# Sorted expert layers: the slot's token is found by one-hot products and its row gathered, where the token's row was scattered to its slot

## Chip, cores and metric

One core of one Trainium2 chip runs the whole program. The metric is the device time of one execution in microseconds (us); for the kernel before, the median of three runs.

## The reference, cut to what matters

`x` has 8 x 256 tokens of 128 numbers. Four times a cross attention and then a feed-forward layer are added to it, each with a gate. The change touches the feed-forward layers 1 and 2, which have eight experts with 512 hidden units:

```python
# layer 1: one expert per token, weighted by its probability
route = softmax(xn @ router_w + router_b); best = argmax(route)
a, g = split(xn @ w1[best], 2);  y = silu(a) * g @ w2[best]
x = x + tanh(g_ffn[1]) * y * max(route)
# layer 2: two experts per token, weighted by the softmax of the two logits
vals, idx = top_k(xn @ gate_w + gate_b, 2); share = softmax(vals)
y_k = gelu(xn @ w1[idx_k] + b1[idx_k]) @ w2[idx_k] + b2[idx_k]
x = x + tanh(g_ffn[2]) * sum_k share_k * y_k
```

`xn` is the layer norm of `x`.

## The kernel before

The five engines have programs of their own and meet at semaphores. The function `sparse_ffn` is called for layer 1 (`gated`, K = 1) and layer 2 (K = 2); below they are stage 1 and stage 2. `x` lies in SBUF as 16 tiles of 128 tokens.

**Sorting.** VectorE and GpSimd make the layer norm (lines 2522 to 2537, 2291), TensorE transposes it and makes the router's logits (2311, 2319). VectorE finds the expert of each token, TensorE counts the tokens of each expert and ranks them (2326 to 2331), and VectorE turns that into a slot number for each token (2593 to 2607). Each expert owns whole tiles of 128 slots; there are NS = 24 tiles in stage 1 and 40 in stage 2, which suffices for every outcome. Their owners are computed in 2608 to 2611 and loaded into TensorE's registers (2356).

**Rows to slots.** A DRAM scratch per layer holds rows of 130 numbers: the normalised token, its number, its share. It is filled with empty rows (number 1.0e6) at the start of the first attention, by 16 transfers of 260 KB on SP's queue (536). After `rows_done`, GpSimd scatters 128 rows at a time with indirect DMAs (2297): 16 in stage 1, 32 in stage 2, where ScalarE first copies the rows (2450) since the second choice has other numbers in its last columns. When all have landed, SP fetches groups of four tiles in slot order (2269), up to three ahead; group `g` goes into buffer `g % 3`.

**Weights.** SP loads the experts one by one into a ring of 2 (stage 1) or 3 (stage 2) raw buffers (2257 to 2263); ScalarE rounds them to f16 (`high`, 2435) and VectorE writes what is left (`low`, 2542, 2544). The first RING experts come before the routing on VectorE, the others after it (2619). In stage 2, VectorE's matrix of shares (2618), its transposition (2337), ScalarE's copy (2452), the product with the second bias (2347) and the addition to `x` (2627) stand there too, and TensorE goes on only when that is added.

**Loop.** NG = 6 or 10 groups of 4 tiles, 4 chunks of 128 hidden units each. TensorE transposes a fetched group (`turn`, 2368), multiplies with the owner's weights (`chunk`, 2376 to 2378) and multiplies back (`result`, 2407 to 2411). ScalarE and VectorE split the transposed rows and the hidden values into two f16 parts each. `turn(g + 2)` comes in the middle of group `g`; every product is three matmuls. In stage 2 a chunk passes VectorE (bias, 2653), ScalarE (gelu 2478, high part 2485) and VectorE (low part, 2661). VectorE copies token numbers and shares out of each fetched group (2636, 2637), ScalarE scales the result by the share (2493, four instructions), and GpSimd scatters it by token number into `results` (2303), four indirect DMAs per group; empty slots are left out by the bound check. Once all have landed, SP brings the results back in four quarters (2275) and VectorE adds them to `x` (2689, 2691).

```python
for g in range(NG):
    pool.wait_ge(token_done, 2 * (g + 1))
    pool.wait_ge(y_done, g + 1)
    for i in range(GT):
        nc.gpsimd.indirect_dma_start(results, ...token_at...)
```

## Time and profile before

| | us |
|---|---|
| three runs | 2479.51, 2480.14, 2485.76 |
| median | 2480.14 |
| profiled execution | 2482.54 |
| its span | 2480.80 |
| PE, DVE, ACT, POOL busy | 2031.9, 1742.9, 1339.0, 531.4 |
| mean granted TensorE clock | 0.893 |

PE is TensorE, PEld its weight loads, DVE VectorE, ACT ScalarE, POOL GpSimd, SP the engine that only issues DMAs; a q behind a name (SPq, PEldq) is that engine's sequencer. Times in rows are us from the span's start unless ns is said. A timeline row has start, duration, engine, line, operation, output<-input, and in brackets how long the engine sat idle before it and what ended that. "xN" is a number of instructions.

### The profile page before, as it was taken

How to read it: one execution, taken by the hardware profiler on the slowest of the kernel's cores; microseconds unless marked ns; L12 is line 12 of the kernel's file. 1: busy time of each engine (PE TensorE's matmuls, PEld its weight loads, DVE VectorE, ACT ScalarE, POOL GpSimd, SP SyncE). 2: the span in 40 equal slices, each digit the busy share in tenths (PEclk: the TensorE clock that was granted, in tenths of full speed). 3: DMA queues.
4: the chain of work that ended last, by engine and by line, in shares of the span. 5: the costliest groups of instructions: out<-in, count | busy, mean ns of one | idle time of the engine just before them, and what ended most of it. 6: DMA issues, size and time to landing. Idle time of an engine off the chain costs nothing. (4 is left out here: it accounts for less than half of the span.)

```text
span 2480.8 us, 47937 instructions
## 1 busy us (share of the span) xinstructions
PE 2031.9 (82%) x17000; PEld 1395.1 (56%) x17001; DVE 1742.9 (70%) x3576; ACT 1339.0 (54%) x1775; POOL 531.4 (21%) x510
## 2 busy tenths in 40 slices
PE   3699636999984949999999999999547389999677
PEld 3434324888864715555555555556436268888544
DVE  2567365888875457788787877876535468888688
ACT  1247314777753416666666666667335257777321
POOL 2100001000002323434443344435433300000010
PEclk9679766999996959999999999999668689999789
DMA  5311100000004010000000000000211100000000
GB/s 143 57 24 11 23 0 1 0 0 0 0 27 120 19 49 9 9 12 9 12 9 11 11 9 12 9 11 4 84 54 40 40 1 0 0 0 0 1 22 24
DMA packets 94870, 53.74 MB, mean 22 GB/s; under 512 B 43517, under 2 KB 88808, under 8 KB 94358
## 3 DMA queue, kind: packets, MB, share of 16 engines
q1 hardware_dynamic: 86516, 42.51, 7.3%
q0 software_dynamic: 3584, 6.36, 0.8%
q10 hardware_dynamic: 4610, 2.71, 0.5%
q8 instruction: 104, 1.70, 0.3%
q14 instruction: 56, 0.46, 0.1%
HBM read 30.16 MB, written 13.75 MB: 18 GB/s over the span
## 5 line engine op out<-in xcount | busy, mean ns | idle before, releaser
L1446 POOL TENSOR_TENSOR aw_p_lo<-aw_p,aw_p_hi 128x512 f16<-128x512 f32 x256 | 303.1, 1184 | 499.6 <-ACT aw_p_hi L1400 499.5
L1482 DVE TENSOR_REDUCE aw_max_part<-ps 128x1 f32<-128x512 f32 x512 | 349.8, 686 | 77.2 <-PE ps L1275 74.4
L1398 ACT ACTIVATE aw_p<-ps 128x1024 f32<-128x1024 f32 x256 | 262.3, 1024 | 260.2 <-PE ps L1307 260.1
L1324 PE MATMUL ps<-ctx_hi_lo,aw_p_hi 128*128 128x194 f16 x2048 | 290.8, 247 | 1.2 <-DVE aw_p_lo L1494 0.7
L1494 DVE TENSOR_TENSOR aw_p_lo<-aw_p,aw_p_hi 128x512 f16<-128x512 f32 x256 | 267.5, 1045 | 22.0 <-ACT aw_p_hi L1400 22.0
L1327 PE MATMUL ps<-ctx_hi_lo,aw_p_lo 128*128 128x97 f16 x2048 | 279.4, 207 | 0.0
L1400 ACT ACTIVATE aw_p_hi<-ps 128x1024 f16<-128x1024 f32 x256 | 260.5, 1018 | 0.0
L1275 PE MATMUL ps<-ctxT_hi,aw_queries 96*128 96x512 f16 x512 | 204.1, 400 | 36.0 <-DVE aw_max_part L1482 35.4
L1327 PEld LDWEIGHTS ps<-ctx_hi_lo,aw_p_lo 128*128 128x128 f16 x2048 | 200.4, 98 | 26.1
L1324 PEld LDWEIGHTS ps<-ctx_hi_lo,aw_p_hi 128*128 128x128 f16 x2048 | 199.7, 98 | 5.0 <-issue 4.0
L1302 PE MATMUL ps<-aw_queries,aw_keys 128*128 128x512 f16 x512 | 194.5, 380 | 0.3 <-ACT aw_p_hi L1400 0.3
L1303 PE MATMUL ps<-aw_queries,aw_keys 128*128 128x512 f16 x512 | 193.9, 379 | 0.0
L1040 ACT ACTIVATE at_p<-ps 128x1024 f32<-128x1024 f32 x128 | 131.1, 1024 | 102.9 <-PE ps L946 102.9
L1098 DVE TENSOR_REDUCE at_neg_max<-ps 128x2 f16<-128x512 f32 x256 | 174.3, 681 | 6.0 <-PE ps L925 5.6
L1122 DVE SCALAR_TENSOR_TENSOR x_res<-ps,at_rden,x_res 128x128 f32<-128x128 f32 x520 | 158.6, 347 | 9.2
L447 POOL TENSOR_TENSOR ln_rstd<-ln_var_eps,neg_half 128x16 f32<-128x16 f32 x6 | 17.6, 2932 | 687.3 <-DVE ln_var_eps L433 653.2
L969 PE MATMUL ps<-C,u_out 97*128 (+1 forms) x1040 | 160.2, 276 | 5.1 <-DVE x_res L1122 5.1
L1128 DVE TENSOR_TENSOR at_p_lo<-at_p,at_p_hi 128x1024 f16<-128x1024 f32 x128 | 155.6, 1216 | 7.9 <-ACT at_p_hi L1042 7.7
L969 PEld LDWEIGHTS ps<-C,u_out 97*128 97x128 f32 x1040 | 136.2, 191 | 11.6 <-DVE x_res L1122 8.3
L956 PE MATMUL ps<-at_p_hi,ctx_hi_lo 128*128 128x256 f16 x512 | 140.9, 275 | 1.1 <-DVE at_p_lo L1128 1.1
L944 PE MATMUL ps<-at_q_hi,ctxT_hi 97*128 97x256 f16 x512 | 141.6, 277 | 0.0
L945 PE MATMUL ps<-at_q_hi,ctxT_lo 96*128 96x256 f16 x512 | 141.5, 276 | 0.0
(377 smaller groups left out, 4687.3 us busy)
## 6 DMA issues: line engine op xcount, KB each, us to landing
sf_weights_raw<-in_L_w SPq DMA_DIRECT2D x24, 256.0 KB, 4.1
slot_scratch<-at_empty_rows SPq DMA_DIRECT2D x16, 260.0 KB, 8.1
sf_fetched<-slot_scratch SPq DMA_DIRECT2D x16, 260.0 KB, 3.0
sf_weights_raw<-in_L_w SPq DMA_DIRECT2D x8, 512.0 KB, 3.8
x_norm<-result_scratch SPq DMA_DIRECT2D x8, 256.0 KB, 4.2
aw_queries<-aw_queries SPq DMA_DIRECT2D x32, 64.0 KB, 1.9
aw_queries<-aw_q_lo SPq DMA_DIRECT2D x32, 64.0 KB, 2.0
raw<-in_L_q SPq DMA_DIRECT2D x3, 512.0 KB, 10.4
```

The lines of the kernel that those rows point to most:

```text
L969: ins = nc.tensor.matmul(ps[:, BANKS[b], t * (CW + 1):(t + 1) * (CW + 1)], M.U[:, upar, (2 * half + t) * P:(2 * half + t + 1) * P], C[:, s ...
L1098: nc.vector.tensor_reduce(nmax[:, par, 2 * k:2 * k + 2], ps[:, BANKS[b], :].rearrange("p (t k) -> p t k", t=2), AX.X, ALU.max, negate=True ...
L1275: nc.tensor.matmul(ps[:, bank, :], S1[0:DC, b % 4, t * P:(t + 1) * P], M.ct_hi[0:DC, kb * QB:(kb + 1) * QB], start=True, stop=True).then_i ...
L1302: nc.tensor.matmul(o, K1[:, ks], S1[:, c, :], start=True, stop=False)
L1303: nc.tensor.matmul(o, K2[:, ks], S2[:, c, :], start=False, stop=False)
L1324: nc.tensor.matmul(ps[:, bank, at:at + 2 * VW - 2], p_hi[:, n % 3, cols], M.cv[:, kt, 0:2 * VW - 2], start=kt == 0 and t % 2 == 0, stop=False,
L1327: ins = nc.tensor.matmul(ps[:, bank, at:at + DA], p_lo[:, n % 3, cols], M.cv[:, kt, 0:DA], start=False, stop=kt == NT - 1, skip_group_chec ...
L1398: nc.scalar.activation(p[:, n % 2, :].rearrange("p (b q) -> p b q", b=2), s, ACT.Exp, scale=1.0 / QS).then_inc(p_done, 1)
L1400: nc.scalar.activation(p_hi[:, n % 3, :].rearrange("p (b q) -> p b q", b=2), s, ACT.Exp, scale=1.0 / QS).then_inc(hi_done, 1)
L1446: nc.gpsimd.tensor_tensor(p_lo[:, n % 3, QB:], p[:, n % 2, QB:], p_hi[:, n % 3, QB:], ALU.subtract).then_inc(lo_b, 1)
L1482: nc.vector.tensor_reduce(mpart[:, b % 2, k:k + 1], ps[:, bank, :], AX.X, ALU.max).then_inc(m_done, 1)
L1494: nc.vector.tensor_tensor(p_lo[:, n % 3, 0:QB], p[:, n % 2, 0:QB], p_hi[:, n % 3, 0:QB], ALU.subtract).then_inc(lo_a, 1)
```

## The change

The rows stay in token order: SP stores the normalised rows to a DRAM scratch `rows`, ahead of the load of expert RING. VectorE cuts each slot number into a tile (`>> 7`) and a place in the tile (`& 127`), and makes two f16 one-hot sets: `in_part` (place) and `in_tile` (tile, times token number + 1). TensorE multiplies them, so that `found` holds token + 1 for each slot, or 0. VectorE makes two address lists: `token_at` (0 for empty slots) and `home_at` (beyond the bound for empty slots, + 2048 for second choices). GpSimd gathers the rows of group `g` by `token_at`, three groups before the loop and group `g + 3` ahead of the scatter of result `g`. The shares are no longer carried with the rows: ScalarE copies the result in one instruction, and VectorE multiplies by the share when it adds. The empty rows, their transfers and ScalarE's copy of the rows go, as do the token and share copies in the loop. Rows have 128 numbers in place of 130, and `combT` shares `M.xt`'s memory. The declarations of semaphores and the slices `0:D` that became `:` are left out here:

```diff
@@ -36,7 +36,7 @@
...
-XW = D + 2
+XW = D
@@ -113,9 +113,8 @@
...
-    M.count = sb("count", [P, 1, 64], F32)
-    M.slots = {n: nc.dram_tensor(f"slot_scratch{n}", [k * P, XW], F32, kind="Internal").ap()
-               for n, k in ((1, 24), (2, 40))}
+    M.count = sb("count", [P, 1, P], F32)
+    M.rows = nc.dram_tensor("row_scratch", [NTOK, D], F32, kind="Internal").ap()
@@ -268,7 +267,7 @@
...
-    link(nc.gpsimd.iota(M.count[:], [[1, 64]], base=0, channel_multiplier=0,
+    link(nc.gpsimd.iota(M.count[:], [[1, P]], base=0, channel_multiplier=0,
@@ -498,8 +497,6 @@
...
-        empty = sb("empty_rows", [P, TQ, XW], F32)
@@ -524,17 +521,9 @@
...
-    nc.gpsimd.memset(empty[:], 0.0).then_inc(empty_zeroed, 1)
-    pool.wait_ge(empty_zeroed, 1)
-    nc.gpsimd.memset(empty[:, :, D:D + 1], 1.0e6).then_inc(empty_done, 1)
...
-    sp.wait_ge(empty_done, 1)
-    for n, k in ((1, 24), (2, 40)):
-        for i in range(k // TQ):
-            sp.dma_start(M.slots[n][i * QB:(i + 1) * QB, :].rearrange("(t p) f -> p t f", p=P), empty[:]
-                         ).then_inc(cleared, 16)
@@ -544,7 +533,6 @@
...
-    sp.wait_ge(cleared, 64 // TQ * 16)
@@ -2177,7 +2165,7 @@
...
-    ps, slots, results = M.ps, M.slots[layer], M.results
+    ps, rows, results = M.ps, M.rows, M.results
@@ -2209,10 +2197,15 @@
...
-        slot_at = sb("slot_at", [P, K, NT], mybir.dt.uint32)
-        fetch = sb("fetched", [P, 3, GT, XW])
-        token_at = sb("token_at", [P, 4, GT], mybir.dt.uint32)
-        share_at = sb("share_at", [P, 4, GT])
+        slot_int, part_int = (sb(n, [P, K, NT], mybir.dt.int32) for n in ("slot_int", "part_int"))
+        slot_part, slot_tile = (sb(n, [P, K * NT]) for n in ("slot_part", "slot_tile"))
+        in_part = sb("in_part", [P, K * NT, P], F16)
+        in_tile = sb("in_tile", [P, K * NT, NS], F16)
+        token1 = sb("token1", [P, NT], F16)
+        found = sb("found", [P, K, NS])
+        token, home, none = (sb(n, [P, NS]) for n in ("token", "home", "none"))
+        token_at, home_at = (sb(n, [P, NS], mybir.dt.uint32) for n in ("token_at", "home_at"))
+        fetch = sb("fetched", [P, 3, GT, D])
@@ -2223,27 +2216,28 @@
...
-            combT = sb("combT", [E, NTOK])
+            combT = M.xt[0:E, :]
...
-        rows = [M.xn, M.xt_rows]
@@ -2256,23 +2250,22 @@
...
+        if e == RING:
+            for q in range(NQ):
+                sp.wait_ge(normed, (q + 1) * TQ)
+                sp.dma_start(rows[q * QB:(q + 1) * QB, :].rearrange("(t p) f -> p t f", p=P),
+                             M.xn[:, q * TQ:(q + 1) * TQ, :]).then_inc(rows_stored, 16)
...
-    sp.wait_ge(scattered, K * NT * 16)
-    for g in range(NG):
-        if g >= 3:
-            sp.wait_ge(s_turned, g - 2)
-            sp.wait_ge(token_done, 2 * (g - 2))
-        sp.dma_start(fetch[:, g % 3], slots[g * QB:(g + 1) * QB, :].rearrange("(t p) f -> p t f", p=P)
-                     ).then_inc(fetched[g % 3], 16)
+    sp.wait_ge(rows_stored, 4 * 16)
...
-            sp.dma_start(sum_of[k][:, q * TQ:(q + 1) * TQ, 0:D],
+            sp.dma_start(sum_of[k][:, q * TQ:(q + 1) * TQ, :],
@@ -2282,25 +2275,35 @@
...
-    nc.gpsimd.iota(M.xn[:, :, D], [[P, NT]], base=0, channel_multiplier=1,
+    nc.gpsimd.iota(token1[:], [[P, NT]], base=1, channel_multiplier=1,
...
-    for k in range(K):
-        pool.wait_ge(rows_done, k + 1)
-        if k:
-            pool.wait_ge(copied, 1)
-        for t in range(NT):
-            nc.gpsimd.indirect_dma_start(slots, bass.IndirectOffsetOnAxis(slot_at[:, k, t:t + 1], 0),
-                                         rows[k][:, t, :], None).then_inc(scattered, 16)
+    pool.wait_ge(places_done, 1)
+    pool.wait_ge(rows_stored, 4 * 16)
...
+    def fetch_group(g):
+        if g >= 3:
+            pool.wait_ge(s_turned, g - 2)
+        for i in range(GT):
+            s = g * GT + i
+            nc.gpsimd.indirect_dma_start(fetch[:, g % 3, i, :], None, rows,
+                                         bass.IndirectOffsetOnAxis(token_at[:, s:s + 1], 0)
+                                         ).then_inc(fetched[g % 3], 16)
...
+    for g in range(3):
+        fetch_group(g)
+    pool.wait_ge(places_done, 2)
...
-        pool.wait_ge(token_done, 2 * (g + 1))
+        if g + 3 < NG:
+            fetch_group(g + 3)
...
-            nc.gpsimd.indirect_dma_start(results, bass.IndirectOffsetOnAxis(token_at[:, g % 4, i:i + 1], 0),
+            s = g * GT + i
+            nc.gpsimd.indirect_dma_start(results, bass.IndirectOffsetOnAxis(home_at[:, s:s + 1], 0),
@@ -2308,7 +2311,7 @@
...
-        ins = nc.tensor.transpose(ps[:, t // TQ, (t % TQ) * P:(t % TQ + 1) * P], M.xn[:, t, 0:D],
+        ins = nc.tensor.transpose(ps[:, t // TQ, (t % TQ) * P:(t % TQ + 1) * P], M.xn[:, t, :],
@@ -2331,6 +2334,15 @@
...
+    pe.wait_ge(tile_done, 1)
+    for k in range(K):
+        for t in range(NT):
+            n = k * NT + t
+            if n % 8 == 0:
+                pe.wait_ge(part_done, n // 8 + 1)
+            ins = nc.tensor.matmul(ps[:, CB, 64 * (k + 1):64 * (k + 1) + NS], in_part[:, n, :],
+                                   in_tile[:, n, :], start=t == 0, stop=t == NT - 1)
+    ins.then_inc(found_done, 1)
@@ -2360,12 +2372,12 @@
...
-        pe.wait_ge(fetched[g % 3], 16 * (g // 3 + 1))
+        pe.wait_ge(fetched[g % 3], GT * 16 * (g // 3 + 1))
...
-            ins = nc.tensor.transpose(ps[:, TB, i * P:(i + 1) * P], fetch[:, g % 3, i, 0:D], M.ident[:])
+            ins = nc.tensor.transpose(ps[:, TB, i * P:(i + 1) * P], fetch[:, g % 3, i, :], M.ident[:])
@@ -2446,10 +2458,8 @@
...
-        act.wait_ge(logits, 1)
-        nc.scalar.activation(M.xt_rows[:, :, 0:D], M.xn[:, :, 0:D], ACT.Copy).then_inc(copied, 1)
...
-        nc.scalar.activation(combT[:].rearrange("e (b t) -> e b t", b=4), ps[0:E, 0:4, :], ACT.Copy
+        nc.scalar.activation(combT.rearrange("e (b t) -> e b t", b=4), ps[0:E, 0:4, :], ACT.Copy
@@ -2486,13 +2496,10 @@
...
-        act.wait_ge(token_done, 2 * (g + 1))
...
-        for i in range(GT):
-            ins = nc.scalar.activation(y_sb[:, g % 2, i, :], ps[:, YB + g % 2, i * D:(i + 1) * D], ACT.Copy,
-                                       scale=share_at[:, g % 4, i:i + 1])
-        ins.then_inc(y_done, 1)
+        nc.scalar.activation(y_sb[:, g % 2].rearrange("p t f -> p (t f)"), ps[:, YB + g % 2, :], ACT.Copy
+                             ).then_inc(y_done, 1)
@@ -2533,7 +2540,7 @@
...
-        V.tensor_scalar(M.xn[:, t, 0:D], M.x[:, t, :], mean[:, t:t + 1], rstd[:, t:t + 1],
+        V.tensor_scalar(M.xn[:, t, :], M.x[:, t, :], mean[:, t:t + 1], rstd[:, t:t + 1],
@@ -2567,7 +2574,7 @@
...
-        V.tensor_scalar(M.xn[:, :, D + 1:D + 2], share[0][:], gate, None, ALU.mult)
+        link(V.tensor_scalar(share[0][:], share[0][:], gate, None, ALU.mult))
@@ -2585,10 +2592,6 @@
...
-        V.tensor_copy(M.xn[:, :, D + 1:D + 2], share[0][:])
-        dve.wait_ge(logits, 1)
-        V.tensor_copy(M.xt_rows[:, :, D + 1:D + 2], share[1][:])
-        V.tensor_scalar(M.xt_rows[:, :, D:D + 1], M.xn[:, :, D:D + 1], float(NTOK), None, ALU.add)
@@ -2604,7 +2607,20 @@
...
-        V.tensor_copy(slot_at[:, k], slot[:, k]).then_inc(rows_done, 1)
+    link(V.tensor_copy(slot_int[:], slot[:]))
+    link(V.tensor_scalar(part_int[:], slot_int[:], P - 1, None, ALU.bitwise_and))
+    link(V.tensor_scalar(slot_int[:], slot_int[:], 7, None, ALU.logical_shift_right))
+    link(V.tensor_copy(slot_part[:], part_int[:].rearrange("p k t -> p (k t)")))
+    link(V.tensor_copy(slot_tile[:], slot_int[:].rearrange("p k t -> p (k t)")))
+    link(V.tensor_tensor(in_tile[:], slot_tile[:].unsqueeze(2).to_broadcast([P, K * NT, NS]),
+                         M.count[:, 0:1, 0:NS].to_broadcast([P, K * NT, NS]), ALU.is_equal))
+    for k in range(K):
+        ins = V.tensor_tensor(in_tile[:, k * NT:(k + 1) * NT], in_tile[:, k * NT:(k + 1) * NT],
+                              token1[:].unsqueeze(2).to_broadcast([P, NT, NS]), ALU.mult)
+    ins.then_inc(tile_done, 1)
+    for n in range(0, K * NT, 8):
+        V.tensor_tensor(in_part[:, n:n + 8, :], slot_part[:, n:n + 8].unsqueeze(2).to_broadcast([P, 8, P]),
+                        M.count[:, 0:1, :].to_broadcast([P, 8, P]), ALU.is_equal).then_inc(part_done, 1)
@@ -2616,6 +2632,19 @@
...
+    dve.wait_ge(found_done, 1)
+    link(V.tensor_copy(found[:], ps[:, CB, 64:64 * (K + 1)].rearrange("p (k s) -> p k s", k=K)[:, :, 0:NS]))
+    whole = found[:, 0, :]
+    if K > 1:
+        link(V.tensor_tensor(token[:], found[:, 0, :], found[:, 1, :], ALU.add))
+        whole = token[:]
+    V.tensor_scalar(token_at[:], whole, -1.0, 0.0, ALU.add, ALU.max).then_inc(places_done, 1)
+    link(V.tensor_scalar(none[:], whole, 0.0, 1.0e6, ALU.is_equal, ALU.mult))
+    link(V.scalar_tensor_tensor(home[:], whole, -1.0, none[:], ALU.add, ALU.add))
+    if K > 1:
+        link(V.tensor_scalar(none[:], found[:, 1, :], 0.0, float(NTOK), ALU.is_gt, ALU.mult))
+        link(V.tensor_tensor(home[:], home[:], none[:], ALU.add))
+    V.tensor_copy(home_at[:], home[:]).then_inc(places_done, 1)
@@ -2630,11 +2659,6 @@
...
-        dve.wait_ge(fetched[g % 3], 16 * (g // 3 + 1))
-        if g >= 4:
-            dve.wait_ge(y_out[g % 2], GT * 16 * ((g - 4) // 2 + 1))
-        V.tensor_copy(token_at[:, g % 4, :], fetch[:, g % 3, :, D]).then_inc(token_done, 1)
-        V.tensor_copy(share_at[:, g % 4, :], fetch[:, g % 3, :, D + 1]).then_inc(token_done, 1)
@@ -2685,10 +2709,14 @@
...
-        t0, t1 = q * TQ, (q + 1) * TQ
-        link(V.tensor_tensor(M.x[:, t0:t1, :], M.x[:, t0:t1, :], sum_of[0][:, t0:t1, 0:D], ALU.add))
+        for t in range(q * TQ, (q + 1) * TQ):
+            V.scalar_tensor_tensor(M.x[:, t, :], sum_of[0][:, t, :], share[0][:, t, :], M.x[:, t, :],
+                                   ALU.mult, ALU.add).then_inc(added, 1)
...
-            V.tensor_tensor(M.x[:, t0:t1, :], M.x[:, t0:t1, :], sum_of[1][:, t0:t1, 0:D], ALU.add)
+            dve.wait_ge(added, (q + 1) * TQ)
+            for t in range(q * TQ, (q + 1) * TQ):
+                V.scalar_tensor_tensor(M.x[:, t, :], sum_of[1][:, t, :], share[1][:, t, :], M.x[:, t, :],
+                                       ALU.mult, ALU.add)
```

## Rows read from the trace of the kernel before

**Rows 1.** Busy time in three stretches, core 0. Columns: stretch, us, busy us by engine (instructions).

```profile
110.00:120.00 10.00, 10.00 (x40) 4.12 (x39) 6.19 (x9) 5.65 (x11) 0.00 (x0) 0.84 1.20 216
810.00:823.00 13.00, 13.00 (x153) 10.47 (x151) 5.91 (x11) 6.25 (x15) 4.02 (x4) 1.00 0.06 20
1855.00:1865.00 10.00, 7.97 (x93) 7.15 (x91) 5.89 (x11) 5.44 (x12) 3.94 (x4) 0.84 0.18 51
```

**Rows 2.** TensorE's waits. Columns: who waited for whom, us in total, times, longest.

```profile
PE ps L2368 <- DMA sf_fetched<-slot_scratch: 59.7, 2, 30.9
```

**Rows 3.** GpSimd in order of time, stage 2: first and last of the 32 scatters.

```profile
1779.54 1.05 POOL L2297 DMA_INDIRECT slot_scratch<-x_norm,sf_slot_at  x1 [18.29 <-DVE sf_slot_at L2607]
...
1819.16 0.96 POOL L2297 DMA_INDIRECT slot_scratch<-x_normT,sf_slot_at  x1 [0.30 <-issue]
```

**Rows 4.** TensorE at the start of stage 2's loop: a timeline row, then rows by line.

```profile
1824.48 1.11 PE L2368 MATMUL ps<-ident,sf_fetched 128*128 128x128 f32 x4 [30.89 <-DMA sf_fetched<-slot_scratch]
...
L2356 PEldq TENSOR_LOAD <-sf_owner_at x2: 1366/1378/1390, 1796.0 to 1797.4; - x2
...
L2376 PE MATMUL ps<-x_normT_hi,sf_weights x7: 268/314/314, 1827.2 to 1830.0; 128*128 128x128 f16 x7
```

**Rows 5.** VectorE in order of time, stage 2, before the loop. Columns: start, us, instruction.

```profile
1779.80 0.18 DVE L2607 CAST sf_slot_at<-sf_slot 128x16 uint32<-128x16 f32 x1
...
1779.88 0.48 DVE L2608 TENSOR_TENSOR sf_past<-sf_tiles_upto,count 128x320 f32<-128x320 f32 x1
...
1781.81 0.29 DVE L2618 TENSOR_TENSOR comb<-sf_exps,sf_logits 128x128 f32<-128x128 f32 x1
...
1798.90 0.74 DVE L2544 TENSOR_TENSOR sf_weights<-sf_weights_raw,sf_weights 128x512 f16<-128x512 f32 x1
```

**Rows 6.** VectorE and TensorE in order of time, stage 1.

```profile
761.23 1.22 DVE L2542 TENSOR_TENSOR sf_weights<-sf_weights_raw,sf_weights 128x1024 f16<-128x1024 f32 x1
...
783.12 0.69 DVE L2544 TENSOR_TENSOR sf_weights<-sf_weights_raw,sf_weights 128x512 f16<-128x512 f32 x1
...
789.46 0.28 PE L2376 MATMUL ps<-x_normT_hi,sf_weights 128*128 128x128 f16 x1 [1.55 <-ACT x_normT_hi L2463]
```

**Rows 7.** Transfers (us to landing), SP's issues, and VectorE writing the rows, stage 2.

```profile
result_scratch<-sf_y,sf_token_at POOLq DMA_INDIRECT x64, 2.3
...
1766.70 0.33 SPq L2261 DMA_DIRECT2D sf_weights_raw<-in_L_w  x1
...
1761.28 4.20 DVE L2536 TENSOR_SCALAR x_norm<-x_res,sf_mean,sf_rstd 128x128 f32<-128x128 f32 x16 [3.03 <-POOL sf_rstd L2291]
```

**Rows 8.** All engines in order of time, inside stage 2's loop.

```profile
1857.87 1.14 ACT L2493 ACTIVATE sf_y<-ps,sf_share_at 128x128 f32<-128x128 f32 x4
...
1868.62 1.12 ACT L2493 ACTIVATE sf_y<-ps,sf_share_at 128x128 f32<-128x128 f32 x4
...
1870.58 0.98 POOL L2303 DMA_INDIRECT result_scratch<-sf_y,sf_token_at  x1 [5.88 <-ACT sf_y L2493]
...
1871.26 0.69 DVE L2661 TENSOR_TENSOR sf_hidden_lo<-sf_hidden,sf_hidden_hi 128x512 f16<-128x512 f32 x1 [1.22 <-ACT sf_hidden_hi L2485]
...
1873.64 0.58 ACT L2463 ACTIVATE x_normT_hi<-ps 128x512 f16<-128x512 f32 x1
...
1874.38 0.68 DVE L2632 TENSOR_TENSOR x_normT_lo<-ps,x_normT_hi 128x512 f16<-128x512 f32 x1
...
1875.12 0.69 DVE L2653 TENSOR_TENSOR sf_silu<-ps,sf_bias 128x512 f32<-128x512 f32 x1
```

**Rows 9.** GpSimd by line and form. Columns: count, busy us, mean ns, idle before it.

```profile
L2303 POOL DMA_INDIRECT result_scratch<-sf_y,sf_token_at x64 | 64.0, 1000 | 159.5 <-ACT sf_y L2493 144.8 <-issue 14.6
...
L2297 POOL DMA_INDIRECT slot_scratch<-x_norm,sf_slot_at x32 | 32.9, 1028 | 45.4 <-DVE sf_slot_at L2607 36.3 <-issue 9.1
...
L2291 POOL TENSOR_TENSOR sf_rstd<-sf_var_eps,neg_half 128x16 f32<-128x16 f32 x2 | 5.8, 2914 | 4.7 <-DVE sf_var_eps L2533 4.7
```

**Rows 10.** VectorE at the end of stage 2: the last addition.

```profile
1961.14 0.69 DVE L2691 TENSOR_TENSOR x_res<-x_res,x_normT 128x512 f32<-128x512 f32 x1
```

More of the change, by code:

```diff
@@ L500, in attention_small_heads @@
         rden = sb("rden", [P, 2, 4 * TQ, 1], F32)
-        empty = sb("empty_rows", [P, TQ, XW], F32)
-        empty_zeroed, empty_done, cleared = sem("empty_zeroed"), sem("empty_done"), sem("slots_cleared")
         k_ready, k_hi, k_done = sem("keys_ready"), sem("keys_hi_done"), sem("keys_done")
@@ L2232, in sparse_ffn @@
         chain, shifted, exp_done = sem("chain"), sem("shifted"), sem("exp_done")
-        picked, ranked, rows_done, owners_done = sem("picked"), sem("ranked"), sem("rows_done"), sem("owners_done")
-        copied, fetched = sem("rows_copied"), [sem(f"fetched{g}") for g in range(3)]
-        s_turned, s_hi, s_lo, token_done = sem("sorted_turned"), sem("sorted_hi"), sem("sorted_lo"), sem("token_done")
+        picked, ranked, owners_done = sem("picked"), sem("ranked"), sem("owners_done")
+        part_done, tile_done, found_done, places_done = sem("part_done"), sem("tile_done"), sem("found"), sem("places_done")
+        added = sem("added")
+        rows_stored = sem("rows_stored")
+        fetched = [nc.alloc_semaphore(f"sf{layer}_fetched{g}") for g in range(3)]
+        s_turned, s_hi, s_lo = sem("sorted_turned"), sem("sorted_hi"), sem("sorted_lo")
         a_ready, silu_done, g_ready, mult_done = sem("a_ready"), sem("silu_done"), sem("g_ready"), sem("mult_done")
@@ L2239, in sparse_ffn @@
         y_ready, y_done = sem("y_ready"), sem("y_done")
-        scattered = nc.alloc_semaphore(f"sf{layer}_scattered")
         y_out = [nc.alloc_semaphore(f"sf{layer}_y_out{i}") for i in range(2)]
```

## The prediction

> **What bounds the kernel now.** I read the table of stretches first, then what TensorE waited for, then the engines' instructions in order of time in the two sorted stages. The first stage (layer 1, 24 slot tiles, 6 groups) runs from about 736 to 885 us, the second (layer 2, 40 tiles, 10 groups) from about 1754 to 1962 us; the rest of the kernel isn't touched but for the clearing of the slots. In the steady part of stage 1 TensorE is busy 13.00 of 13 us; in that of stage 2 it is busy 7.97 of 10 [rows 1]. TensorE's wait for a fetched group is 59.7 us in two pieces, one of 30.9 us [rows 2]; the two are the starts of the two stages.
>
> In stage 2 the 32 scatters run back to back from 1779.54 to past 1819.16 us, and the first group reaches TensorE at 1824.48 [rows 3, 4]. The converted weights were ready at 1798.90 + 0.74 = 1799.64 us [rows 5]. So the scatter alone holds the start, by some 25 us. In stage 1 it is otherwise: the last weights are subtracted at 783.12 + 0.69 = 783.81, and the first product starts at 789.46 [rows 6]. The scatter holds that start by only 5.6 us.
>
> **Stage 1, the start.** The gathers replace the scatter, but the weights now end later. On VectorE, ahead of the subtraction at 761.23 on which the ring of two raw buffers hangs [rows 6], stand: 5 small linked steps at 0.21 us (a 0.18 us cast and the gap of a link [rows 5]), 1.05 us; a comparison over 384 elements, 0.59; a product over as many, 0.50; two comparisons of 128x1024, the second and later at 1.14 (1.22 of duration [rows 6], 0.08 overlapped), 2.28; copying the found tokens and making both address lists, 0.95. Less one cast, 5.3 us. The sizes between are scaled from 0.29 us for 128 and 0.48 for 320 elements [rows 5], some 1 ns each. The TensorE products (16 and 32, at 0.03 to 0.1 us) lie under the last comparison and the owner's steps. The chain subtract, load, convert, subtract then repeats for the later experts, so all of the 5.3 us arrives: weights at 789.1 instead of 783.8. The first gathers begin at some 766.3 and the first group lands near 772.5, so it waits for the weights. The products start at 789.1 in place of 789.46: -0.3 us. SP's four row stores go out as the rows are normalised, ahead of the next weight load that had to wait anyway (in stage 2 the rows are written from 1761.28 for 4.2 us, the next load is issued at 1766.70 [rows 7]): nothing, at most the 1 to 2 us by which that load lands later, and its conversion has several us of slack.
>
> **Stage 2, the start.** The slots are known at 1779.72, 0.08 before the cast's 1779.80. Then: small steps 1.05; a comparison over 1280 elements 1.5; two products over 640, 1.5; four comparisons of 128x1024, 4.6. Together 8.6 us, less 0.15 for casts gone: 8.5. They stand ahead of the step that makes the shares' matrix (1781.81 [rows 5]), and from there the old chain follows: transposes, copy, bias products, addition to x, and TensorE's register loads, whose last ends at 1797.4 + 1.38 = 1798.8 [rows 4]. With 8.5 it is 1807.3. Weights come at 1799.64 + 8.5 = 1808.1, but the first transposes only need the registers. From the first transpose to the first product it took 1827.2 - 1824.48 = 2.7 us [rows 4]. The new start is 1807.4 + 2.7 = 1810.1 against 1827.2: **-17.0 us**. The gathers: the one-hots end at 1788.3, the owner's steps and the shares' matrix take 2.2 as before (1779.88 to 1782.10 [rows 5]), three steps make the addresses by 1791.2, the first gather starts at 1791.5, pace 0.96 + 0.30 = 1.26 us as the scatters; four land by 1791.5 + 3.8 + 2.3 = 1797.6 [rows 3, 7], the twelfth by 1807.7. TensorE wants the third group only near 1816.
>
> **The loops.** Stage 1 is TensorE's, nothing there. Stage 2 has a period of 1868.62 - 1857.87 = 10.75 us, set by VectorE and ScalarE handing each chunk to and fro; the two small copies behind the subtraction (1874.38 to the next chunk's 1875.12, 0.74 of which 0.60 is the subtraction) stand in it [rows 8]. Without them 0.14 x 10 = -1.4 us. Is GpSimd then the bound? Four scatters at 1.000 + 0.30 and four gathers make 5.2 + 5.05 = 10.25 us, with the gathers at the 0.96 of the scatter of rows; at the 1.028 us mean of the contended ones 10.5 [rows 9]. Period 10.6: it fits, with hardly any room. A scatter starts some 0.85 us behind its result (1868.62 + 1.12 to 1870.58 [rows 8]), the next gather group lands 0.85 + 5.2 + 3.8 + 2.3 = 12.1 us behind it, and ScalarE wants that group's transposes some 14 us behind it (result of the group two before at about 1859, high part at 1873.64 [rows 8]): about 2 us of room.
>
> The gather is the unknown price. From below, nothing: a gather that costs no GpSimd time gives no more, since the loop isn't GpSimd's. From above, 2.91 us, the dearest GpSimd instruction of these stages [rows 9]. I take 0.96, since the instruction is the same kind with the same 128 rows.
>
> **The ends.** The result becomes one 128x512 ScalarE instruction, 0.6 us, where four took 1.12 to 1.14 [rows 8]: -0.5 in each stage, on the last group only. The share now comes in with the additions: four instructions per quarter (4.20 / 16 = 0.26 us each [rows 7]) for one of 0.69 [rows 10]. In stage 2 eight for two, plus a wait: 2.2 for some 1.4 us, and the last three quarters queue up, since they arrive 1.7 us apart: +1.8. Stage 1: +0.6. The clearing of the slots (16 transfers at 109 us) lies under a TensorE busy 10.00 of 10 us [rows 1]: nothing; taking it away uncovers nothing either.
>
> **Sum.** Stage 1: -0.3 - 0.5 + 0.6 = -0.2. Stage 2: -17.0 - 1.4 - 0.5 + 1.8 = -17.1. Together -17.3 us. The profiled execution took 2482.54 us (span 2480.80, 1.74 around it) and would take 2465.2. The median of the runs is 2480.14, 2.4 below it, so the forecast is **2462.8 us**. A measurement can tell about 0.3%, 7.4 us, from no change.
>
> **A rule against the change.** The scatter that starts at 1870.58 takes 0.98 us though a subtraction with two SBUF inputs runs on VectorE from 1871.26 to 1871.95, and the mean of all 64 is 1.000 [rows 8, 9]; they aren't held up. The Trainium skill, SBUF — State Buffer, section "SBUF: two separate sides", says that a DMA from GpSimd's queue is starved while VectorE holds the port pair that the two share, and that one from SP or ScalarE is immune; the change moves the fetch from SP to GpSimd. By that rule each gather would wait for up to a VectorE instruction, which is the third rival; by the row the sum stands.
>
> **Rivals.** (1) GpSimd becomes the bound of stage 2's loop, mildly. Six cycles hold gathers (groups 4 to 9). With d us more per gather the loss is 6 x (4d - 0.4) - 2: 3 us at d = 0.3, 10 at 0.6, so 2466 to 2473. For it: 10.25 of 10.6 us. Against: the scatters' even pace. 0.14. (2) The building of the one-hots is cheaper than one element per ns, since its outputs, and the product's inputs, are 16-bit. At half price, -2 in stage 1 and -4 in stage 2: 2456 to 2457. Against: the comparisons read f32, and the 16-bit-output subtraction of 128x1024 takes 1.22 us [rows 6]. 0.10. (3) Gathers held up by VectorE for one 0.69 us instruction each: 6 x (2.76 - 0.4) - 2 = 12, or a building that costs double (+5 and +8): 2475 to 2476, no measurable change. 0.08. (4) **Slower**: the gather itself is much dearer than the scatter, on GpSimd in stage 2's loop. The gain of 17.3 is used up at d = 0.85, a gather of 1.8 us; at 2.0 us the loss is 6 x 3.8 - 2 plus 3 at the third group, 24, so 2487; at the upper bound of 2.91, 6 x 7.4 - 2 plus 13 gives about 2518. 0.06. That the change doesn't do what it says is no case of weight: addresses feed the gathers directly. The forecast has 0.62.
>
> **Range.** Forecast, (1) and (2) hold 0.86 and lie on the fast side; they span 2455 to 2474. Faster by over 0.3% has 0.86, no change 0.08 (case 3), slower 0.06.
>
> **What would show it.** Right: TensorE's wait at stage 2's start ends near 1807 us; the first product of stage 1 is within 1 us of 789.5; gathers of 0.96 to 1.03 us; period of stage 2 10.6 us; VectorE's comparisons of 128x1024 at 1.2 us. Wrong: gathers over 1.1 us, with TensorE waiting for fetched groups inside the loop; a stage 1 that starts late because the weights came later than 789; or a last addition of stage 2 more than 2 us further behind its transfers.

## The result, and the profile after

The changed kernel takes 2467.4 us (median of 4 runs, 2466.46 to 2468.09) against 2480.4 for the kernel before on the same chip: ratio 0.9945, 95% interval 0.9927 to 0.9963, 13.0 us faster. The forecast was 2462.8, 17.3 faster. The profiled execution took 2466.46 us (span 2464.7); the pair of profiles differs by 16.1, since the one of before lies 2.2 us above its median and the one of after is its lowest run.

TensorE's waits for a fetched group, and the table of stretches with one in the steady part of stage 2; they answer to [rows 1, 2]:

```profile
PE ps L2380 <- DMA sf_fetched<-row_scratch,sf_token_at: 23.5, 7, 11.5
```

```profile
1855.00:1865.00 10.00, 8.18 (x99) 6.63 (x98) 5.66 (x9) 5.00 (x10) 7.80 (x8) 1.00 0.19 53
```

Two waits of 59.7 us have become seven of 23.5: the 30.9 us one is gone, the 11.5 us one stands in stage 1 beside the weights, and the small ones, 1.5 to 3.0 us each, are new and lie inside stage 2's loop. GpSimd is busy 7.80 of 10 us, and the rest is its 0.30 us between instructions.

The start of stage 2, by engine in order of time, answers to [rows 3 to 5]:

```profile
1790.48 0.29 DVE L2634 TENSOR_TENSOR comb<-sf_exps,sf_logits 128x128 f32<-128x128 f32 x1
1791.19 0.18 DVE L2641 TENSOR_SCALAR sf_token_at<-sf_token 128x40 uint32<-128x40 f32 x1
...
1791.66 1.04 POOL L2293 DMA_INDIRECT sf_fetched<-row_scratch,sf_token_at  x1 [33.03 <-DVE sf_token_at L2641]
...
1806.14 0.95 POOL L2293 DMA_INDIRECT sf_fetched<-row_scratch,sf_token_at  x1 [0.30 <-issue]
...
1796.36 5.73 PE L2359 MATMUL ps<-sf_b,x_normT 8*128 8x128 f32 x32 [0.84 <-ACT x_normT L2462]
1807.30 1.09 PE L2380 MATMUL ps<-ident,sf_fetched 128*128 128x128 f32 x4 [5.21 <-issue]
1810.04 0.29 PE L2388 MATMUL ps<-x_normT_hi,sf_weights 128*128 128x128 f16 x1 [1.65 <-DVE x_normT_lo L2661]
```

The shares' matrix comes at 1790.48 where it came at 1781.81, the first product at 1810.04 where it came at 1827.2 (each from its own span's start; stage 2 begins at 1754.68 here and at 1757.29 before). The first group had long been fetched: TensorE came to it late, from its register loads ("issue").

The start of stage 1, VectorE and then TensorE, answers to [rows 6]:

```profile
759.07 2.35 DVE L2622 TENSOR_TENSOR sf_in_part<-sf_slot_part,count 128x1024 f16<-128x1024 f32 x2
...
763.03 1.21 DVE L2549 TENSOR_TENSOR sf_weights<-sf_weights_raw,sf_weights 128x1024 f16<-128x1024 f32 x1
...
785.44 0.28 PE L2388 MATMUL ps<-x_normT_hi,sf_weights 128*128 128x128 f16 x1 [11.01 <-DVE x_normT_lo L2661]
```

GpSimd by line, and six of its instructions inside stage 2's loop, answer to [rows 8, 9]:

```profile
L2293 POOL DMA_INDIRECT sf_fetched<-row_scratch,sf_token_at x64 | 67.8, 1059 | 74.1 <-DVE sf_token_at L2641 53.5 <-issue 16.8 <-PE ps L2380 2.4
L2306 POOL DMA_INDIRECT result_scratch<-sf_y,sf_home_at x64 | 65.1, 1018 | 95.5 <-ACT sf_y L2501 79.4 <-issue 16.1
...
1856.35 0.98 POOL L2306 DMA_INDIRECT result_scratch<-sf_y,sf_home_at  x1 [0.30 <-issue]
1857.64 0.99 POOL L2293 DMA_INDIRECT sf_fetched<-row_scratch,sf_token_at  x1 [0.30 <-issue]
1858.93 1.33 POOL L2293 DMA_INDIRECT sf_fetched<-row_scratch,sf_token_at  x1 [0.30 <-issue]
1860.57 0.95 POOL L2293 DMA_INDIRECT sf_fetched<-row_scratch,sf_token_at  x1 [0.30 <-issue]
1861.83 0.94 POOL L2293 DMA_INDIRECT sf_fetched<-row_scratch,sf_token_at  x1 [0.30 <-ACT sf_y L2501]
1863.08 1.02 POOL L2306 DMA_INDIRECT result_scratch<-sf_y,sf_home_at  x1 [0.30 <-issue]
```

From 1830.67 to 1894.5 us GpSimd is never idle for longer than 0.31 us. Most instructions take 0.94 to 1.02, but one in most groups takes 1.33 to 1.44. A gather lands 3.4 us after its issue, the median of both stages (the prediction used the scatter's 2.3).

The end of stage 2, first two and last group of VectorE's additions, answers to [rows 10]:

```profile
1936.01 1.14 DVE L2713 SCALAR_TENSOR_TENSOR x_res<-x_norm,sf_share,x_res 128x128 f32<-128x128 f32 x4 [16.05 <-DMA x_normT<-result_scratch]
1937.18 1.14 DVE L2718 SCALAR_TENSOR_TENSOR x_res<-x_normT,sf_share,x_res 128x128 f32<-128x128 f32 x4
...
1944.73 1.14 DVE L2718 SCALAR_TENSOR_TENSOR x_res<-x_normT,sf_share,x_res 128x128 f32<-128x128 f32 x4
```

### The profile page after: what moved, and what is told of

Read it like the earlier page. It is cut to its first block and busy times, and to the rows that moved or that the text cites. A ratio compares the mean times of both kernels' runs of the same rounds, so it can differ in the third digit from the quotient of the medians.

```text
span 2464.7 us, 47969 instructions
## 1 busy us (share of the span) xinstructions
PE 2036.8 (83%) x17049; PEld 1397.4 (57%) x17049; DVE 1759.7 (71%) x3608; ACT 1328.3 (54%) x1726; POOL 551.0 (22%) x524
## 5 line engine op out<-in xcount | busy, mean ns | idle before, releaser
L1291 PE MATMUL ps<-aw_queries,aw_keys 128*128 128x512 f16 x512 | 194.9, 381 | 0.0
L957 PEld LDWEIGHTS ps<-C,u_out 97*128 97x128 f32 x1040 | 136.5, 191 | 11.6 <-DVE x_res L1110 8.2
## 6 DMA issues: line engine op xcount, KB each, us to landing
raw<-in_L_q SPq DMA_DIRECT2D x3, 512.0 KB, 10.7
raw<-in_L_o SPq DMA_DIRECT2D x3, 512.0 KB, 12.5
```

Of the source, the lines that this page charges most:

```text
L957: ins = nc.tensor.matmul(ps[:, BANKS[b], t * (CW + 1):(t + 1) * (CW + 1)], M.U[:, upar, (2 * half + t) * P:(2 * half + t + 1) * P], C[:, s ...
L1291: nc.tensor.matmul(o, K2[:, ks], S2[:, c, :], start=False, stop=False)
```

## The experiments

**Two profiles don't make a difference of 3 us.** In the pair of profiles stage 1 had gained 3.2 us, far more than forecast. So each kernel was run again, and the change by halves; in `new_layer1` and `new_layer2` one stage has the new `sparse_ffn`, the other the old one with its slots' clearing:

```diff
-                sparse_ffn(nc, M, d, n)
+                (sparse_ffn_new if n == 1 else sparse_ffn)(nc, M, d, n)   # new_layer2: n == 2
```

`before_again`: 

> The kernel before, once more, for its profile. In its first profile the router's matmuls took 6.83 us in stage 1 and 4.16 us in stage 2; in the changed kernel's it is the other way round, which accounts for 3.0 us gained in stage 1 and 2.8 us lost in stage 2. Theory A: the clock's fall meets the one or the other stage by chance of the run, so this profile may show any pair, and the pair belongs to no part of the change. Theory B: it belongs to the kernel, so 6.83 in stage 1 and 4.16 in stage 2 again.

`after_again`: 

> The changed kernel, once more, for a closer interval: 2467 us, 13.0 below the kernel before, with 2 us either way. Theory A: its router's matmuls may take 6.83 or 4.16 us in either stage. Theory B: 4.16 in stage 1 and 6.83 in stage 2 again.

`new_layer1`: 

> Stage 1 (sorted layer with one expert a token) in the new form, stage 2 in the old one, whose 40 groups' slots are still cleared ahead. The prediction's sum: 0.2 us faster than before, 2480 us with 2 either way. Rival: the 3.2 us that the changed kernel's profile shows in stage 1 belong to the change, 2477 us.

`new_layer2`: 

> Stage 2 in the new form, stage 1 in the old one. The prediction's sum: 17.1 us faster, 2463 us. From the changed kernel's profile, where the copies out of the loop gave nothing back in it and the end of the stage took 2.4 us longer: 13 to 14 us faster, 2466 to 2467 us. Rival: if 3 us of the gain are stage 1's, this one gains 10 us only, 2470 us.

Measured, against 2480.0 for the kernel before (17 runs): `after_again` 2465.9 (ratio 0.9948, 0.9933 to 0.9964), `new_layer1` 2481.1 (0.9998, 0.9987 to 1.001), `new_layer2` 2466.4 (0.9940, 0.9924 to 0.9955). So the gain is stage 2's, within some 3 us. The rest is read from the timelines. Each stage is counted from VectorE's first small step of the layer norm (`sf_a`); "length" is to the power on GpSimd in the next layer norm, "tail" from the last result to there:

| profile | st. 1: router | product | length | st. 2: router | product | 9 periods | tail | length |
|---|---|---|---|---|---|---|---|---|
| before | 15.4 | 50.6 | 150.4 | 12.6 | 70.0 | 95.7 | 23.7 | 209.1 |
| before_again | 12.6 | 49.4 | 149.1 | 12.6 | 69.9 | 95.8 | 24.1 | 209.6 |
| new_layer1 | 12.4 | 47.0 | 147.2 | 15.3 | 73.1 | 95.4 | 24.1 | 211.9 |
| new_layer2 | 12.7 | 48.3 | 147.9 | 12.5 | 54.1 | 96.0 | 25.3 | 194.6 |
| after | 12.3 | 47.0 | 147.1 | 15.3 | 55.4 | 95.6 | 25.6 | 195.8 |
| after_again | 12.4 | 46.8 | 146.9 | 12.9 | 54.4 | 96.2 | 25.3 | 194.9 |

"Router" is the end of the router's 32 products, 12.3 to 12.9 or 15.3 to 15.4 us. Their busy time in two stretches of the first profile of before, and of after (columns: stretch, us, TensorE and weight loads, granted clock, DMA share, GB/s):

```profile
747.00:755.00 8.00, 6.83 (x32) 6.94 (x32) 0.50 0.59 189
1763.00:1771.00 8.00, 4.16 (x32) 4.16 (x32) 0.71 0.32 92
```

```profile
747.00:755.00 8.00, 3.79 (x32) 3.70 (x31) 0.69 0.83 247
1763.00:1771.00 8.00, 6.83 (x32) 6.93 (x32) 0.50 0.84 236
```

At the lower level (0.50, 1.2 GHz) the same products take 6.83 us, with the clock raised on the way 4.16 or less. Which stage meets it changes from one profile to the next: all of `before_again`, `after_again` and `new_layer2` had it in neither. Theory A holds, and 3 us in stage 1 and -2.8 in stage 2 of the pair are chance.

With the router alike, stage 2's length goes from 209.3 to 194.7: -14.6 us, of which -15.7 by the first product, -0.6 from it to the first result, +0.3 in the nine periods, +1.4 in the tail. Stage 1's first product moves from 49.4 and 48.3 to 46.5 to 47.3 where the router was quick, and not at all where it was late (50.6 before; 50.3, 50.6 and 50.4 in three later profiles of the new form): 0 to -1.9 (the difference of the means), forecast -0.3.

**Is GpSimd the bound of stage 2's loop?** One gather more, and two buffers more:

```diff
+                    if not gated and g >= 3:                    # five_gathers
+                        nc.gpsimd.indirect_dma_start(spare[:, g % 2, :], None, rows, ...)
-        fetch = sb("fetched", [P, 3, GT, D])                    # five_buffers
+        FR = 3 if gated else 5
+        fetch = sb("fetched", [P, FR, GT, D])                   # and 3 -> FR in its uses
```

`five_gathers`: 

> The changed kernel with one gather more for each of groups 3 to 9 of stage 2, into a spare buffer that nothing reads: 1.26 us more on GpSimd in each of the six cycles that hold gathers. If GpSimd has become the bound of those cycles, they go from 10.6 to 11.9 us and the kernel takes 6 x 1.26 = 7.5 us more, 2473.5. Rival, by the prediction's room (VectorE and ScalarE bound, 0.35 us a cycle and 2 us at the start to spare): 6 x 0.9 - 2 = 3.5 us more, 2469.5. If GpSimd has nothing to do with it: no change.

`five_buffers`: 

> The changed kernel with five fetch buffers in stage 2 in place of three, so that 24 of the 40 gathers are done before the first scatter and the rest are asked for five groups ahead. If GpSimd bounds the loop of stage 2, the nine periods between the first and the last result go from 95.6 to 96.2 us down to 94.3 (the 1.4 us that the prediction put on the two copies come out), 2 us less in all, and TensorE's waits inside the loop are gone. Rival: the handing to and fro of VectorE and ScalarE holds the period at 10.6 whatever the copies did, and nothing changes.

Measured: `five_gathers` 2471.5 (0.9963, 0.9950 to 0.9977), 5.6 more than `after_again`'s median; nine periods of 102.8 us in place of 95.9 (mean of the three profiles), 6.9 more, against 7.5 and 3.5 expected. `five_buffers` 2464.0 (0.9937, 0.9915 to 0.9959), nine periods of 95.1, 0.9 less; by time alone it can't be told from the changed kernel (and in its profile a stretch ahead of stage 1, which the change doesn't touch, is some 6 us shorter than in the others). TensorE's waits inside the loop, and two results on ScalarE, first of `five_gathers`:

```profile
PE ps L2389 <- DMA sf_fetched<-row_scratch,sf_token_at: 19.5, 6, 4.9
...
1885.52 0.58 ACT L2510 ACTIVATE sf_y<-ps 128x512 f32<-128x512 f32 x1
1899.50 0.60 ACT L2510 ACTIVATE sf_y<-ps 128x512 f32<-128x512 f32 x1
```

and of `five_buffers`:

```profile
PE ps L2420 <- DVE sf_hidden_lo L2686: 19.3, 9, 3.4
...
1843.21 0.58 ACT L2502 ACTIVATE sf_y<-ps 128x512 f32<-128x512 f32 x1
1853.84 0.58 ACT L2502 ACTIVATE sf_y<-ps 128x512 f32<-128x512 f32 x1
```

With five gathers a period reaches 14.0 us. With five buffers no wait for a fetched group is left in the loop (the 19.3 us are TensorE's for VectorE, the old bound). In the changed kernel the first periods are 10.60 to 10.64 too, and GpSimd just keeps that pace: in `after` the last gathers of groups 4 to 8 start at 1840.56, 1851.19, 1861.83, 1872.62 and 1883.26, 10.63 to 10.79 apart. About the sixth result one period slips to 11.6 to 12.3, and there the rows come late. The last gather of group 8 and TensorE's use of that group, in `after`:

```profile
1883.26 0.94 POOL L2293 DMA_INDIRECT sf_fetched<-row_scratch,sf_token_at  x1 [0.30 <-ACT sf_y L2501]
...
1887.41 0.90 PE L2380 MATMUL ps<-ident,sf_fetched 128*128 128x128 f32 x3 [3.04 <-DMA sf_fetched<-row_scratch,sf_token_at]
```

From the last gather's start to TensorE's it takes 4.15 us here, and 2.5 to 3.3 for groups 4 to 7. In `after_again` it is 4.19 for group 8, in `new_layer2` 4.45 for group 7, and each time this wait lies inside the period that slips. Why these rows land later was not tried. The loss varies with it: over all seven profiles of the changed loop, those below included, the nine periods take 95.6 to 97.5 us, mean 96.4; with five buffers they take 95.1 here and 94.7 in `best` below. So GpSimd has nothing to spare: rival 1, at its mildest.

**The shares in the additions.** This kernel leaves the weighting by the shares out:

```diff
-                    for t in range(q * TQ, (q + 1) * TQ):
-                        V.scalar_tensor_tensor(M.x[:, t, :], sum_of[0][:, t, :], share[0][:, t, :], M.x[:, t, :], ...)
+                    link(V.tensor_tensor(M.x[:, t0:t1, :], M.x[:, t0:t1, :], sum_of[0][:, t0:t1, :], ALU.add))
```

> The changed kernel with the shares left out: the rows that come back are added as they are, one 128x512 addition each, as before the change (the experts' results are thus not weighted). From the last result of a stage to the next stage's first GpSimd instruction it takes 25.4 us in stage 2 with the shares and 24.0 before; the prediction put 1.8 us on the additions of stage 2 and 0.6 on those of stage 1. So 1.4 to 1.8 less in stage 2 and 0.4 to 0.8 less in stage 1, 2464 us. Rival: the end is set by the transfers and nothing changes.

Measured 2461.1 (0.9928, 0.9909 to 0.9947). The tail of stage 2 is 23.2 us, 2.2 less than with the shares (and 0.5 to 1.0 less than before, by the quicker result), that of stage 1 18.8 against 19.1 to 19.3, 0.4 less. Its additions of stage 2, first and last:

```profile
1932.41 0.69 DVE L2713 TENSOR_TENSOR x_res<-x_res,x_norm 128x512 f32<-128x512 f32 x1 [15.88 <-DMA x_normT<-result_scratch]
...
1939.08 0.69 DVE L2715 TENSOR_TENSOR x_res<-x_res,x_normT 128x512 f32<-128x512 f32 x1
```

7.4 us from the first addition's start to the last one's end, 9.9 with the shares (1936.01 to 1945.87 above). The medians differ by 4.8 us (2465.9 to 2461.1), of which the tails show 2.6; the expected sizes hold. In the profiles stage 1's loop is shorter too, 60.5 us for 61.2 and 61.5, by which more below; the rest isn't explained.

**The clearing.** 16 transfers of zeros into a spare tensor:

```diff
+                for i in range(16):
+                    sp.dma_start(M.spare[i * QB:(i + 1) * QB, :].rearrange("(t p) f -> p t f", p=P), empty[:])
```

> The changed kernel with the 16 transfers of 256 KB of zeros kept, into a spare tensor of DRAM, in the first attention. The prediction put the clearing at nothing, TensorE being busy 10.00 of 10 us there: no change within 1 us. Rival: the transfers cost the attention something, which the change took away, and this kernel is 1 to 2 us slower than the changed one.

Measured 2468.0 (0.9948, 0.9928 to 0.9968). Stage 1 starts at 737.3 us, with the changed kernel's two profiles at 738.5 and 737.7. VectorE's 201st instruction, behind these transfers, starts at 198.2 us in all three. No cost shows; the medians, 2468.0 and 2465.9, can't tell one of 1 or 2 us.

**What the one-hots delay.** Two reorderings, and both with the five buffers:

```diff
                 for k in range(K):                              # order2, VectorE
                     ...
+                link(V.tensor_tensor(past[:], ...))
+                ...
+                    V.tensor_tensor(M.comb[:, :, 0:E], ex[:], v[:], ALU.add).then_inc(comb_done, 1)
                 link(V.tensor_copy(slot_int[:], slot[:]))
                 ...
-                link(V.tensor_tensor(past[:], ...))
-                ...
                     ins.then_inc(bias_ready, 1)                 # order2, TensorE
+                    places(pe)                                  # the one-hot products
                     pe.wait_ge(combT_done, 1)
+                if gated:                                       # low_early, VectorE
+                    for e in range(RING, 2 * RING):
+                        low(e)
                 dve.wait_ge(ranked, 1)
```

`order2` (its register loads stand ahead of all that): 

> The changed kernel with the order of stage 2's start altered: VectorE makes the owners and the shares' matrix ahead of the one-hots, TensorE takes the one-hot products between the transposes and bias products and the products with b2, and its register loads stand first. If the 8.5 us of one-hots delay the start because they stand ahead of the shares' matrix, they now run beside TensorE's and ScalarE's part of that chain, and the first product comes 48 to 49 us behind the stage's first small steps, where it came at 54.1 to 54.4: 5 to 6 us faster than the changed kernel, some 2461 us. Rival: the weights hold the start then (the last of them is subtracted 52 us in now), and 2 us at most are gained.

`low_early`: 

> The changed kernel with two experts' subtractions in stage 1 moved ahead of the ranking steps, so that the ring of two raw buffers refills while VectorE builds the one-hots. If the weights' chain holds the start of stage 1, as the prediction has it (the one-hots' 5.3 us arrive in it in full), the first product comes at 42 to 43 us in place of 46.9, and the kernel is 4 to 5 us faster than the changed one, some 2462 us. Rival: the gathers hold the start of stage 1; they begin 4 us later here, so the product comes 4 us later, 2470 us.

`best`: 

> Both reorderings and the five fetch buffers of stage 2 together. If the three are independent their gains add up: 5.5, 4.5 and 1.5 to 2 us off 2466.5, 2455 us; the first product at 42 to 43 us in stage 1, at 48 to 49 in stage 2, and nine periods of 95.1 us in its loop. Rival: an earlier start of stage 2 leaves less time for the gathers ahead of the first scatter, the loop falls back to 95.9 us, and 2457 is what is left.

Measured against 2481.6 before: `order2` 2459.4 (0.9911, 0.9896 to 0.9926), `low_early` 2463.3 (0.9916, 0.9902 to 0.9929), `best` 2454.7 (0.9893, 0.9878 to 0.9908), 26.9 us faster than before. TensorE's first products, of `low_early` in stage 1 (stage from 737.81):

```profile
781.17 0.28 PE L2388 MATMUL ps<-x_normT_hi,sf_weights 128*128 128x128 f16 x1 [2.88 <-DVE x_normT_lo L2664]
```

and of `best` in stage 2 (stage from 1748.47):

```profile
1792.55 1.08 PE L2385 MATMUL ps<-ident,sf_fetched 128*128 128x128 f32 x4 [2.85 <-DMA sf_fetched<-row_scratch,sf_token_at]
1796.48 0.28 PE L2393 MATMUL ps<-x_normT_hi,sf_weights 128*128 128x128 f16 x1 [2.85 <-DVE x_normT_lo L2669]
```

That is 43.4 us, with the late router, for 50.3 to 50.6 (7 less, 4 to 5 expected), and 48.0 for 54.1 to 54.4 (6.2 less, 5 to 6 expected). `order2` has 50.3 with the late router for 55.4 to 56.8. The kernel's own time is less clear for `low_early`: its median is 2.7 to 4.1 us below the changed kernel's two, its ratio 7 to 8 us. Both rivals fall: it is the place of the one-hots in VectorE's order that costs, the weights in stage 1 and the shares' chain in stage 2. But `order2` moved TensorE's register loads too. From the products with b2 to the first transposes it took 5.21 us in the changed kernel ("issue") and takes 2.85 in `best`, where the gathers now hold the start; so up to 2.4 of the 6.2 us may be the loads'. The two weren't tried apart. In `best` the nine periods are 94.7 us: the third gain isn't lost.

**The two copies.** The last kernel put two 128x4 copies back into the loop of `five_buffers`:

```diff
+                    V.tensor_copy(idle_at[:, g % 4, :], found[:, 0, 0:GT])
+                    V.tensor_copy(idle_share[:, g % 4, :], found[:, 0, 0:GT])
```

> The kernel with five fetch buffers in stage 2, where TensorE waits for no fetched group in the loop, and with two small 128x4 copies put back behind VectorE's subtraction of each group's low part, as they stood before the change (they read a tile that doesn't change and nothing reads them). The prediction says that the two copies stand in the period of stage 2: the periods go back from 10.63 to 10.77 us and the nine from 95.1 to 96.3. Rival: the period is set by something else and the copies are hidden; periods of 10.63 and nine of 95.1.

Measured: one run of 2499.9 us, 36 above `five_buffers`, which neither theory explains. VectorE, where it wasn't kept waiting, and TensorE in the same loop:

```profile
1857.70 0.69 DVE L2689 TENSOR_TENSOR sf_hidden_lo<-sf_hidden,sf_hidden_hi 128x512 f16<-128x512 f32 x1 [1.22 <-ACT sf_hidden_hi L2497]
1858.31 0.68 DVE L2663 TENSOR_TENSOR x_normT_lo<-ps,x_normT_hi 128x512 f16<-128x512 f32 x1
1858.91 0.41 DVE L2664 CAST sf_idle_at<-sf_found 128x4 uint32<-128x4 f32 x1
1858.98 0.35 DVE L2665 COPY sf_idle_share<-sf_found 128x4 f32<-128x4 f32 x1
...
1860.95 0.69 DVE L2689 TENSOR_TENSOR sf_hidden_lo<-sf_hidden,sf_hidden_hi 128x512 f16<-128x512 f32 x1 [1.22 <-ACT sf_hidden_hi L2497]
...
1864.17 0.22 PE L2391 MATMUL ps<-x_normT_lo,sf_weights 128*128 128x128 f16 x1 [0.52 <-issue]
1865.57 0.26 PE L2392 MATMUL ps<-x_normT_hi,sf_weights 128*128 128x128 f16 x1 [1.17 <-issue]
```

From one low part to the next, past the two copies, it takes 1860.95 - 1857.70 = 3.25 us; in `five_buffers` the same stretch (1837.73 to 1840.83) takes 3.10. It recurs once a group, at 3.25 in six of the eight groups here and at 3.10 in seven of eight there; `before`, with its own two copies, has 3.25 in all eight, `after` 3.10 to 3.11 in seven. So the copies do stand in the period, with 0.15 us. The 36 us are another matter: TensorE stood between its products without a wait, 0.3 to 2.5 us at a time, in the loops of both stages (the copies are made in both). The other profiles of the changed kernel, of `five_buffers` and of `best` have no such gaps between products. Whether this one execution or this program does that is open; it was run once.

## Why the prediction was right or wrong

**Stage 2's start**, forecast -17.0, measured -15.7 with the router alike. The one-hots were sized right: the shares' matrix moved from 24.5 us behind the stage's start to 33.0 (router alike), the 8.5 forecast. What failed is "from there the old chain follows" at the old durations. In seven of the nine profiles with this start of stage 2, all but the first and `copies_back`, the 32 products with b2 run at the lower clock. TensorE in `after_again`, with the stretch's granted clock (columns as in [rows 1]):

```profile
1790.01 1.93 PE L2354 MATMUL ps<-sf_owned,sf_b 8*128 8x40 f32 x8
1792.04 7.19 PE L2359 MATMUL ps<-sf_b,x_normT 8*128 8x128 f32 x32
...
1790.00:1799.00 9.00, 8.90 (x41) 8.68 (x40) 2.73 (x5) 5.67 (x9) 7.09 (x7) 0.50 0.54 148
```

and before:

```profile
1785.66 1.09 PE L2342 MATMUL ps<-sf_owned,sf_b 8*128 8x40 f32 x8
1787.68 5.91 PE L2347 MATMUL ps<-sf_b,sf_combT 8*128 8x128 f32 x32 [0.94 <-ACT sf_combT L2452]
...
1786.00:1794.00 8.00, 6.65 (x39) 6.24 (x38) 3.11 (x6) 4.75 (x7) 6.17 (x7) 0.69 0.47 130
```

7.19 for 5.91 is the 1.3 us. In the first profile of after they took 5.73, and its first product, less 2.8 for the router, came at 52.6, where the forecast put it (52.8). TensorE's longest wait beside the one-hots is 8.4 us in all nine, the two quick ones included, for 5.3 us in the old form; in `order2` and `best` it is 7.1, and the products took 7.12 and 7.19. So that wait alone doesn't decide the clock, and its cause stays open.

**Stage 2's loop**, forecast -1.4, measured +0.3 (+0.6 by the mean of the seven profiles). This is the step that failed, in three parts. First, the copies' 0.14 was right for one period (0.15 by the last experiment; 10.60 to 10.64 at first for 10.75 to 10.78 in both profiles of before), but not ten times: even in `five_buffers` the last four periods are 10.92, 11.03, 10.58 and 9.45, where before has 10.91, 10.89, 10.55 and 9.39. Second, "it fits, with hardly any room" took 10.25 us for GpSimd's cycle, from scatters that were hardly held up. Eight instructions at 0.98 + 0.30 make 10.24, and in the new loop one per cycle is held up by 0.35 to 0.46, so 10.6 to 10.7 against a period of 10.62. Third, the rows of a group were to land 2.3 us behind its last gather; to TensorE's start they took 2.5 to 3.4 for most groups in the three profiles, 4.45 once for group 7 and 3.9 to 5.3 for groups 8 and 9, which is most of the 2 us of room and at times more than all of it. Price: 1.7 us, of which `five_buffers` gets 0.9 back.

**The ends**: the quicker result 0.6 (forecast 0.5), read from last result to last group's first scatter; the additions +2.0 in stage 2 (forecast 1.8) from there to the last addition, since four take 1.14 and not 4 x 0.26 = 1.04, and +0.6 in stage 1 as forecast. `plain_add` shows 2.2 and 0.4.

**Stage 1**: forecast -0.2, `new_layer1` can't be told from before; right. The periods of its loop, at which the prediction put nothing, are a small open end: all five take 60.6 us in the three profiles with the old stage 1, but 61.1 to 61.6 in eight of the ten undisturbed ones with the new (60.5 and 60.6 in the others). The difference is in the last period, 8.8 or 9.4 to 9.8, and wasn't followed further. The clock granted there was 1.00 in `before_again` (858 to 868 us) and 0.67 in `after_again` (856 to 866). The clearing: right at nothing. **The gather's price**: 0.94 to 1.02 where it isn't held up, as taken; rival 4 falls, and rival 3 in its size. Rival 2 (cheaper one-hots) falls with 2.35 us for two comparisons (2.28 forecast).

**The sum.** By like profiles 14.6 + 0 to 1.9, by the medians 13.0 and 14.1, against 17.3. Of stage 2's 17.1 - 14.6 = 2.5 us the clock has 1.3, the loop 1.7 and the ends 0.1, and 0.6 came back between the first product and the first result, which no step had. The result, 2466 to 2467, is at the near edge of rival 1 (2466 to 2473, given 0.14) rather than at the forecast; the mechanism was that rival's, with 0.1 us more per gather (mean 1.06) where it asked for 0.3, because its room of 0.4 us per cycle and 2 at the start was counted too large. That the time still came near the forecast is not the loop's doing: the start, 15.7 of the 17.0 us, carries it.

## What to carry over

An engine whose own cycle is 97% of the period isn't covered by it: count its instructions at what they cost beside the new neighbours and its data at the latest landing, and let it run further ahead if buffers allow. When slots or indices are computed on the busiest engine, place that work beside another engine's chain and not ahead of it; here that brought the first product 7 us forward in stage 1 and, with the register loads moved as well, 6 in stage 2. Before a few microseconds between two profiles are explained, take both again and compare the stretches that the change doesn't touch.
